# Graph attention over blocks of eight tiles: every third unit's exponent is formed in a PSUM bank, and rows of targets and sides reach all partitions through DRAM

## Chip, cores and metric

One core of one Trainium2 chip. The metric is the device time of one launch, in microseconds (us). Engines: TensorE (PE; PEld is its weight load), VectorE (DVE), ScalarE (ACT), GpSimd (POOL), SyncE (SP, which only issues DMAs here).

## The reference, cut to what matters

6250 nodes with 128 features, 200,000 edges sorted by target. An edge network with a maximum over each target's edges comes first, then a layer norm, then two attention layers of this form (h = x @ W; every node also has an edge to itself), then a layer norm.

```python
a_src = h @ att_src;  a_dst = h @ att_dst
e = a_src[src] + a_dst[dst]
e = jnp.where(e > 0, e, 0.2 * e)
m = segment_max(e, dst)
ex = jnp.exp(e - m[dst])
out = segment_sum(ex[:, None] * h[src], dst) / segment_sum(ex, dst) + bias
```

## The kernel before, in words

The first 2.5 ms are the edge network; the change leaves its loop alone. While it runs, a second thread fills `counts`: edges and nodes are laid out in 62 tiles of 128 targets (rows), and for every tile, every source chunk of 128 nodes and every pair the table holds how many edges join them. So an attention layer has no gather of features: it multiplies dense 128 x 128 tiles of weights by the projected features `tab`.

The 62 tiles go in blocks (`supers`) of 8, the last of 6. A block has 49 **units**, one for each chunk h of 128 sources. Unit u of a block i needs, for 8 x 128 = 1024 target columns at once, exp(max(s + x, 0.2 s + y)), where s is the source's score (one per partition), and x and y are the target's two sides (its score, and 0.2 of it, each less its maximum), as rows that every partition holds: `x_rows`, `y_rows`. Per unit:

- ScalarE, `exponents(u)`: two passes of 1024 columns, exp(x + s) into `e_ring` (L864) and exp(y + 0.2 s) into `f_ring` (L867).
- VectorE, `weigh(u)`: their maximum (L1395); `mask(u)`: capped and multiplied by the counts, into `a_ring`, three deep (L1406).
- TensorE, `add_unit(u)`: eight fp32 products with `tab[:, h]`, added over the 49 units into six PSUM banks, three for each of two blocks in turn (L1758).

Every engine runs its own list, written by loops over u: VectorE weighs u + 1, then masks u. SyncE loads `counts` in pieces of seven units.

Between the units each engine has side work of two kinds, placed by the unit's number h in its block.

*Flushes* of the block before (`flushed`): tile after tile, every five units, TensorE spreads the tile's targets over the partitions (`spread_target`, through the helper at L1559), VectorE compares them (`same_target`, L1416 and L1419), ScalarE copies the tile's sums (`copy_sums`, L873), TensorE adds them up by runs (`sum_runs`, L1777 and L1780), ScalarE copies these (`copy_runs`, L880) and GpSimd stores them. `spread_target` of the next tile waits for `copy_runs`. TensorE's steps are at h = 2 + 5t and 5 + 5t, VectorE's `DVE_AHEAD` and ScalarE's `ACT_AHEAD` units later in their lists.

*Windows* of the block after (`spread_round`, `window_hots`, `copy_round`): SyncE loads `windows`, the sides of 128 consecutive targets per tile, from a table in DRAM (L532). TensorE spreads the targets (helper at L1559), VectorE makes one-hots of them (L1387), TensorE multiplies the two sides, each spread over all partitions, by the one-hots (L1747) and ScalarE copies the results into `x_rows` and `y_rows` (L855): six rounds of four tiles. The sides come in two parts: chunks 0 to 7 before the units, the others in block 0 (`sides_of(1)` after unit 14, `copy_sides(1)`, L1373, after unit 17), because GpSimd gathers the node's maxima one chunk at a time.

## Time and profile before

| | us |
|---|---|
| Median of 3 runs (lowest, highest) | 4994.77 (4974.24, 5006.46) |
| Profiled execution, its own time | 4974.88 |
| Its span | 4973.6 |
| First and last mask, layer 0 | 2730.8, about 3660 |
| First and last mask, layer 1 | 3985.8, 4915.4 |
| Full block of 49 units | 118 to 121 |

| Engine | busy us | share of the span |
|---|---|---|
| PE | 4123.7 | 83% |
| PEld | 3663.1 | 74% |
| DVE | 3968.5 | 80% |
| ACT | 2804.2 | 56% |
| POOL | 2201.4 | 44% |

A row of a group gives the line in the kernel, the engine and operation, out<-in by the program's names, shapes, the count, busy time and mean duration of one, then the idle time of the engine just before such instructions and what ended it. In the stretches, 3330.7 to 3449.9 is block 5 of layer 0 and 3567.6 to 3660.0 its block 7, of six tiles. Durations of neighbours overlap: an instruction's row ends when its results are written, and the next one starts earlier. So the distance between two starts tells what an engine spends on one. An fp32 product is two records on PE.

### The profile page before, as it was taken

To read this page: it belongs to the slowest core of one execution; us is meant where nothing else is said; L and a number is where in the kernel's file an instruction comes from. 1 tells how busy PE (TensorE), PEld (TensorE's weight loads), DVE (VectorE), ACT (ScalarE), POOL (GpSimd) and SP (SyncE) were. 2 spreads that over 40 slices of the span, in tenths; PEclk is the share of its full clock that TensorE was granted. 3 is DMA by queue.
4 is the path that set the end of the run, shared out by engine and by line. 5 is a ranking of instruction groups with operands and counts; after the bars stand their busy time and mean duration, and the time that the engine had idled before them with its cause. 6 is when DMAs were issued, how large, how long until landed. Compare 5 with 4: busy or idle time off the path is not lost. (4 is left out here: it accounts for less than half of the span.)

```text
span 4973.6 us, 98581 instructions
## 1 busy us (share of the span) xinstructions
PE 4123.7 (83%) x35974; PEld 3663.1 (74%) x35974; DVE 3968.5 (80%) x6028; ACT 2804.2 (56%) x3925; POOL 2201.4 (44%) x2117
## 2 busy tenths in 40 slices
PE   4588888888888888888596888888889788888884
PEld 3477777777777777776474888888877578888884
DVE  4477677777677777765685999999978699999998
ACT  2244444444444444443301899999960089999997
POOL 7777777777777777777302100111120120011121
PEclk7799999999999999998797999999999899999997
DMA  5578677778777777777474211222237512222222
GB/s 174 156 201 228 199 212 216 216 210 222 201 215 216 215 211 218 217 204 200 111 238 145 54 57 57 68 61 62 62 69 241 171 46 59 63 61 61 68 58 58
DMA packets 774547, 721.12 MB, mean 145 GB/s; under 512 B 106779, under 2 KB 642387, under 8 KB 774220
## 3 DMA queue, kind: packets, MB, share of 16 engines
q10 hardware_dynamic: 383570, 310.71, 23.0%
q1 hardware_dynamic: 322714, 271.27, 18.4%
q0 software_dynamic: 67936, 135.03, 9.1%
q8 instruction: 174, 2.85, 0.3%
q14 instruction: 153, 1.25, 0.1%
HBM read 539.16 MB, written 177.56 MB: 144 GB/s over the span
## 5 line engine op out<-in xcount | busy, mean ns | idle before, releaser
L599 POOL DMA_INDIRECT ring_a<-Q_table,late x1563 | 1657.9, 1061 | 477.3 <-issue 466.5
L1758 PE MATMUL ps<-tab_flat,ring_b 128*128 128x129 f32 x12152 | 1502.5, 282 | 75.8 <-DVE ring_b L1406 73.3
L1758 PEld LDWEIGHTS ps<-tab_flat,ring_b 128*128 128x128 f32 x12152 | 1438.9, 197 | 117.6 <-DVE ring_b L1406 115.5
L1395 DVE TENSOR_TENSOR work<-work 128x1024 f32<-128x1024 f32 (+1 forms) x784 | 930.4, 1187 | 43.2 <-ACT work L867 39.9
L864 ACT ACTIVATE work<-work,scores 128x1024 f32<-128x1024 f32 (+1 forms) x784 | 879.6, 1122 | 148.6 <-DVE ring_b L1406 125.8
L1406 DVE SCALAR_TENSOR_TENSOR ring_b<-work,ring_a 128x1024 f32<-128x1024 f32 (+1 forms) x784 | 928.1, 1184 | 3.2 <-PE ps L1758 2.7
L1629 PEld LDWEIGHTS ps<-work,tab_flat 128*128 128x128 bf16 x7936 | 795.7, 142 | 179.7 <-issue 174.8
L1629 PE MATMUL ps<-work,tab_flat 128*128 128x49 bf16 x7936 | 875.0, 273 | 0.0
L867 ACT ACTIVATE work<-work,slope_src 128x1024 f32<-128x1024 f32 (+1 forms) x784 | 868.1, 1107 | 0.0
L1144 DVE TENSOR_TENSOR_SCAN work<-ring_b,work,ps 128x512 f32<-128x512 bf16 x391 | 497.9, 1273 | 446.8 <-PE ps L1602 445.1
L1171 DVE TENSOR_TENSOR tab_flat<-digit_of,ring_b 128x1280 bf16<-128x1280 bf16 x806 | 645.3, 801 | 175.3 <-PE ps L1629 174.0
L766 ACT ACTIVATE ring_a<-ps 128x490 uint8<-128x490 f32 x806 | 480.7, 597 | 537.2 <-PE ps L1629 517.7
L656 POOL DMA_DIRECT2D run_rows<-ring_b x124 | 67.7, 546 | 1577.1 <-ACT ring_b L880 1552.9
L1591 PE MATMUL ps<-ident,ring_a 128*128 128x128 f32 x1563 | 462.9, 296 | 350.6 <-issue 187.2
L714 ACT ACTIVATE work<-ps 128x512 f32<-128x512 f32 x392 | 234.3, 598 | 750.1 <-PE ps L1592 744.2
L1592 PE MATMUL ps<-work 128*128 128x128 f32 x3126 | 592.9, 292 | 0.0
L1591 PEld LDWEIGHTS ps<-ident,ring_a 128*128 128x128 f32 x1563 | 237.3, 152 | 396.9 <-issue 308.8
L1592 PEld LDWEIGHTS ps<-work 128*128 128x128 f32 x3126 | 526.6, 211 | 0.3 <-issue 0.3
L1602 PE MATMUL ps<-work,W 128*128 128x512 f32 (+1 forms) x784 | 437.6, 641 | 0.0
L648 POOL DMA_INDIRECT node_tops<-run_tops,end_i x98 | 116.8, 1192 | 536.5 <-DMA run_tops<-late 507.2
L855 ACT ACTIVATE work<-ps 128x512 f32<-128x512 f32 x64 | 36.1, 564 | 524.9 <-PE ps L1747 524.9
L1173 DVE TENSOR_TENSOR work<-column_of,ring_b 128x490 bf16<-128x490 bf16 x806 | 325.0, 403 | 0.0
(267 smaller groups left out, 4475.3 us busy)
## 6 DMA issues: line engine op xcount, KB each, us to landing
work<-low_rows SPq DMA_DIRECT2D x312, 320.0 KB, 4.1
ring_b<-rank_rows ACTq DMA_DIRECT2D x194, 512.0 KB
run_max<-tab_flat ACTq DMA_DIRECT2D x194, 512.0 KB
ring_a<-counts SPq DMA_DIRECT2D x98, 896.0 KB, 5.1
work<-P_compact SPq DMA_DIRECT2D x787, 64.0 KB
work<-P_compact ACTq DMA_DIRECT2D x776, 64.0 KB
counts<-ring_a ACTq DMA_DIRECT2D x62, 784.0 KB
ring_a<-Q_table,late POOLq DMA_INDIRECT x1563
```

The source lines that it names most:

```text
L599: pool.indirect_dma_start(out=q_ring[:, g % RING, j - j0, :], out_offset=None, in_=Q_table, in_offset=bass.IndirectOffsetOnAxis(ap=srcT_i[ ...
L766: scalar.activation(count_tile[:, tau % 2, :, r0:r1], bank[:, 0:(r1 - r0) * NB].rearrange("p (r h) -> p h r", h=NB), ACT.Copy).then_inc(ba ...
L864: scalar.activation(e_ring[:, u % 3, 0:n], x_rows[:, i % 2, 0:n], ACT.Exp, bias=scores[:, h, 0:1])
L867: scalar.activation(f_ring[:, u % 2, 0:n], y_rows[:, i % 2, 0:n], ACT.Exp, bias=slope_src[:, h:h + 1]).then_inc(exped, 1)
L1144: vector.tensor_tensor_scan(scanned[:, b, 0:n * P], b_ring[:, g % RINGB, 1, a * P:(a + n) * P], ps[2 + b][:, 0:n * P], initial, ALU.add, A ...
L1171: vector.tensor_tensor(hot_rows[:, slot, :, 0:r1 - r0], digit_of[:, :, 0:r1 - r0], low_key[:, tau % 2, r0:r1].unsqueeze(1).to_broadcast([P ...
L1395: vector.tensor_tensor(e_ring[:, u % 3, 0:n], e_ring[:, u % 3, 0:n], f_ring[:, u % 2, 0:n], ALU.max).then_inc(weighed, 1)
L1406: vector.scalar_tensor_tensor(out=a_ring[:, u % RINGA, 0:n].rearrange("p (k e) -> p k e", e=P), in0=e_ring[:, u % 3, 0:n].rearrange("p (k ...
L1591: tensor.matmul(piece, lhsT=q_ring[:, g % RING, a + c, :], rhs=ident[:, :], start=True, stop=False, is_transpose=True)
L1592: m = tensor.matmul(piece, lhsT=w_ring[:, g % RING, a + c, :], rhs=onto[:, i % 3, c * P:(c + 1) * P], start=False, stop=True)
L1629: m = tensor.matmul(bank[:, k * NB:(k + 1) * NB], lhsT=hot_rows[:, hot_slot[b], :, k], rhs=hot_cols[:, hot_slot[b], :, k], start=True, sto ...
L1758: m = tensor.matmul(sums_of(tau), lhsT=a_ring[:, u % RINGA, (tau - a) * P:(tau - a + 1) * P], rhs=tab[:, h, 0:F + 1], start=(h == 0 and (t ...
```

## The change

Of the 49 units of a block, those with h = 1, 4, 7, ... (16) are **banked**, the other 33 **direct**.

A *direct* unit uses exp(max(x + 0.8 s, y) + 0.2 s), the same value: VectorE forms x + 0.8 s and the maximum with y in one instruction (`weigh`, two units ahead now), ScalarE does one exp of 1024 columns in place, VectorE masks.

A *banked* unit uses exp(relu(x - y + 0.8 s) + y + 0.2 s). In halves of 512 columns and in PSUM bank 5 alone, ScalarE writes relu (`begin_bank`, L957 of the new kernel), TensorE adds y on all partitions as a product of ones with three bf16 parts of the row y (`add_to_bank`, L1961), and ScalarE writes the exp to SBUF (`exponents_of_bank`, L965); VectorE only masks. Two halves make five turns of the bank, counted by `bank_turned`. The sums of units now use banks 0 to 4, so `copy_sums` takes the first three tiles of a block at once, right after its last unit, and `sums_sb` is three deep.

The windows of blocks 1 to 7: the targets, transposed once and stored to `target_rows`, are loaded to all partitions (`load_targets`); VectorE compares them in SBUF (`equal_targets`) and splits the window's side into three bf16 parts (`split_window`, nine small instructions); TensorE multiplies parts and both sides by the one-hots with five columns of weights (`spread_parts`, L1938); ScalarE copies three rows of parts and, through `row_stage`, stores the two sides to `row_table` (`copy_parts`), from where they are loaded to all partitions (`load_rows`); VectorE subtracts y from x (`split_rows`). Block 0 keeps its six rounds and gets two more for the parts.

In ScalarE's list, in the middle of a block with a window step. Before (L864 and L867 are a unit's two exps):

```order
L867 ACTIVATE work<-work,slope_src 128x1024
L864 ACTIVATE work<-work,scores 128x1024
L867 ACTIVATE work<-work,slope_src 128x1024
L880 ACTIVATE ring_b<-ps 128x129
L864 ACTIVATE work<-work,scores 128x1024
L867 ACTIVATE work<-work,slope_src 128x1024
L873 ACTIVATE ring_b<-ps 128x129
```

And now (L957 relu into the bank, L920 a direct unit's exp, L965 exp out of the bank, L936 and L937 copies of parts and sides, L982 copied runs):

```order
L957 ACTIVATE ps<-work,steep_src 128x512
L920 ACTIVATE work<-work,slope_src 128x1024
L965 ACTIVATE work<-ps,slope_src 128x512
L957 ACTIVATE ps<-work,steep_src 128x512
L920 ACTIVATE work<-work,slope_src 128x1024
L965 ACTIVATE work<-ps,slope_src 128x512
L936 ACTIVATE pair<-ps 3x512
L937 ACTIVATE digit_of<-ps 5x512
L939 DMA row_table<-digit_of 2x512
L982 ACTIVATE ring_b<-ps 128x129
```

Three units are six passes, of which four are halves, where they were six full ones; the second direct unit's exp stands behind the first half's exp.

In TensorE's list, the same block. Before (L1758 units, L1559 a spread, L1777 and L1780 runs, L1747 windows):

```order
L1777 MATMUL ps<-ring_b 128x129
L1780 MATMUL ps<-ring_b 128x129
L1758 MATMUL ps<-tab_flat,ring_b 128x129 x16
L1747 MATMUL ps<-ring_b,windows 128x128 x4
L1559 MATMUL ps<-ident,v_target 128x128
L1758 MATMUL ps<-tab_flat,ring_b 128x129 x24
```

And now (L1951 units, L1961 adds, L1735 a spread, L1979 and L1982 runs, L1938 parts):

```order
L1735 MATMUL ps<-ident,v_target 128x128
L1951 MATMUL ps<-tab_flat,ring_b 128x129 x16
L1961 MATMUL ps<-pair,ones_b 128x512
L1938 MATMUL ps<-ring_b,part_f 5x128 x4
L1951 MATMUL ps<-tab_flat,ring_b 128x129 x8
L1961 MATMUL ps<-pair,ones_b 128x512
L1979 MATMUL ps<-ring_b 128x129
L1982 MATMUL ps<-ring_b 128x129
```

An add stands behind the unit three (second half) or four (first half) ahead of the unit it is for.

In VectorE's list (L1576 masks, L1564 the pass ahead of them, L1586 and L1589 a flush):

```order
L1576 SCALAR_TENSOR_TENSOR ring_b<-ring_b,ring_a 128x1024
L1586 SCALAR_TENSOR_TENSOR ring_b<-ps,v_target,tri 128x128
L1589 SCALAR_TENSOR_TENSOR ring_b<-ps,v_target,last_col 128x128
L1564 SCALAR_TENSOR_TENSOR work<-work,steep_src 128x1024
L1576 SCALAR_TENSOR_TENSOR ring_b<-work,ring_a 128x1024 x2
L1564 SCALAR_TENSOR_TENSOR work<-work,steep_src 128x1024
L1576 SCALAR_TENSOR_TENSOR ring_b<-work,ring_a 128x1024
L1564 SCALAR_TENSOR_TENSOR work<-work,steep_src 128x1024
```

Three units are five passes; before, L1395 and L1406 took turns, six.

The diff, cut to its core:

```diff
-    REST_AT, REST_XY_AT = 14, 16
-    XY_AT, XY_STEP, FLUSH_AT, FLUSH_STEP, ACT_AHEAD, DVE_AHEAD = 4, 4, 2, 5, 6, 3
+    ROUNDS_X, COPIES_X, BANKS, ZBANK, PARTS = 8, 6, 5, 5, 3
+    REST_AT, REST_XY_AT, SPREAD_AT = 14, 18, 46
+    XY_AT, FLUSH_AT, FLUSH_STEP, ACT_AHEAD, DVE_AHEAD = 4, 2, 5, 3, 2
...
+        y_parts = [pair[0:PARTS, 0, 0:FD], digit_a[0:PARTS, 0:FD]]
+
+        def e_slot(u):
+
+            return e_last if u % 4 == 3 else e_first[:, u % 4, :]
...
-            bank = PER * (at % 2) + j // PER
+            bank = (PER * at + j // PER) % BANKS
...
+        def in_bank(u):
+
+            return u % NB % 3 == 1
...
-                    if q - RINGC - 1 < NS:
-                        load_windows_of(q - RINGC - 1)
+                    if q == RINGC + 2:
+                        load_windows_of(1)
+                    elif q > LOADS and q % LOADS == 2 and q // LOADS + 1 < NS:
+                        load_windows_of(q // LOADS + 1)
...
                 def exponents(u):
                     i, h = divmod(u, NB)
                     n = (supers[i][1] - supers[i][0]) * P
-                    if h == 0:
-                        scalar.wait_ge(window_copied, 4 * (layer * NS + i + 1))
-                    if layer or u >= 3:
-                        scalar.wait_ge(masked, unit0 + max(u - 2, 0))
-                    scalar.activation(e_ring[:, u % 3, 0:n], x_rows[:, i % 2, 0:n], ACT.Exp, bias=scores[:, h, 0:1])
-                    if u >= 2:
-                        scalar.wait_ge(weighed, unit0 + u - 1)
-                    scalar.activation(f_ring[:, u % 2, 0:n], y_rows[:, i % 2, 0:n], ACT.Exp, bias=slope_src[:, h:h + 1]).then_inc(exped, 1)
+                    scalar.wait_ge(weighed, layer * NC + direct_until(u + 1))
+                    scalar.activation(e_slot(u)[:, 0:n], e_slot(u)[:, 0:n], ACT.Exp, bias=slope_src[:, h:h + 1]).then_inc(exped, 1)
+
+                def load_targets(i):
+                    first, n = supers[i][0] * P, (supers[i][1] - supers[i][0]) * P
+                    scalar.wait_ge(window_spread, spreads(layer, i))
+                    scalar.dma_start(window_hot.rearrange("p k e -> p (k e)")[:, 0:n],
+                                     target_rows[:, first:first + n].to_broadcast([P, n])).then_inc(targets_landed, 16)
+
+                def copy_parts(i, half):
+                    c, n, at = halves_of(i)[half]
+                    scalar.wait_ge(window_spread, spreads(layer, i) + half + 1)
+                    if half == 0 and i >= 2:
+                        scalar.wait_ge(bank_turned, layer * TURNS + 1 + 5 * banked_until((i - 1) * NB))
+                    scalar.activation(y_parts[i % 2][:, c:c + n], ps[6][0:PARTS, 0:n], ACT.Copy)
+                    scalar.activation(row_stage[:, 0:n], ps[6][0:PARTS + 2, 0:n], ACT.Copy).then_inc(window_copied, 1)
+                    scalar.wait_ge(window_copied, copies(layer, i) + half + 1)
+                    scalar.dma_start(row_table[:, at:at + n], row_stage[PARTS:PARTS + 2, 0:n]).then_inc(rows_stored, 16)
+
+                def load_rows(i, half):
+                    c, n, at = halves_of(i)[half]
+                    scalar.wait_ge(rows_stored, stored(i, half))
+                    if half == 0 and i >= 2:
+                        scalar.wait_ge(weighed, layer * NC + direct_until((i - 1) * NB))
+                    for a, rows in enumerate((x_rows, y_rows)):
+                        scalar.dma_start(rows[:, i % 2, c:c + n], row_table[a:a + 1, at:at + n].to_broadcast([P, n])).then_inc(rows_landed, 16)
+
+                def begin_bank(u, half):
+                    i, h = divmod(u, NB)
+                    columns, n, turns = z_half(u, half)
+                    if half == 0:
+                        scalar.wait_ge(window_split, 2 * (layer * NS + i) + 2)
+                    scalar.wait_ge(bank_turned, layer * TURNS + turns)
+                    if half == 0 and banked_until(u):
+                        scalar.wait_ge(exped, unit0 + max(x for x in range(u) if in_bank(x)) + 1)
+                    scalar.activation(ps[ZBANK][:, 0:n], r_rows[:, i % 2, columns], ACT.Relu, bias=steep_src[:, h:h + 1]).then_inc(bank_turned, 1)
+
+                def exponents_of_bank(u, half):
+                    i, h = divmod(u, NB)
+                    columns, n, turns = z_half(u, half)
+                    if half == 0 and (layer or u >= 4):
+                        scalar.wait_ge(masked, unit0 + max(u - 3, 0))
+                    scalar.wait_ge(bank_turned, layer * TURNS + turns + 2)
+                    one = scalar.activation(e_slot(u)[:, columns], ps[ZBANK][:, 0:n], ACT.Exp, bias=slope_src[:, h:h + 1])
+                    one.then_inc(exped if half else bank_turned, 1)
...
+                    if u == 0:
+                        begin_bank(1, 0)
+                        exponents_of_bank(1, 0)
+                        begin_bank(1, 1)
+                    if u + 2 < UNITS and in_bank(u + 2):
+                        begin_bank(u + 2, 0)
+                    if not in_bank(u):
+                        exponents(u)
+                    if u + 2 < UNITS and in_bank(u + 2):
+                        exponents_of_bank(u + 2, 0)
+                        begin_bank(u + 2, 1)
+                    if u + 1 < UNITS and in_bank(u + 1):
+                        exponents_of_bank(u + 1, 1)
+                    if i and h == 1:
+                        for tau in range(supers[i - 1][0], supers[i - 1][0] + PER):
+                            copy_sums(tau)
+                    if rows_at(i + 1, h) == 0:
+                        load_targets(i + 1)
+                    if rows_at(i + 1, h) == 8:
+                        copy_parts(i + 1, 0)
+                    if rows_at(i + 1, h) == 12:
+                        load_rows(i + 1, 0)
+                        copy_parts(i + 1, 1)
+                    if rows_at(i + 1, h) == 16:
+                        load_rows(i + 1, 1)
...
+                def equal_targets(i):
+
+                    first, e = supers[i]
+                    vector.wait_ge(targets_landed, 16 * (layer * (NS - 1) + i))
+                    for j in range(e - first):
+                        vector.tensor_scalar(window_hot[:, j, :], window_hot[:, j, :], window_col[:, first + j:first + j + 1], None,
+                                             ALU.is_equal).then_inc(dve.up(), 1)
+
+                def split_window(i):
+
+                    first, n = supers[i][0], supers[i][1] - supers[i][0]
+                    column = windows[:, first:first + n, 1]
+                    vector.wait_ge(windows_landed[i % 2], windows_value(layer, i))
+                    if layer or i:
+                        vector.wait_ge(window_spread, spreads(layer, i))
+                    for a in range(PARTS):
+                        rest = part_rest[:, a - 1, 0:n] if a else column
+                        vector.tensor_copy(part_b[:, a, 0:n], rest).then_inc(dve.up(), 1)
+                        vector.wait_ge(dve.sem, dve.n)
+                        one = vector.tensor_copy(part_f[:, 0:n, a], part_b[:, a, 0:n])
+                        if a == 0:
+                            vector.tensor_copy(part_f[:, 0:n, PARTS:PARTS + 2], windows[:, first:first + n, :])
+                        if a + 1 < PARTS:
+                            vector.tensor_tensor(part_rest[:, a, 0:n], rest, part_b[:, a, 0:n], ALU.subtract).then_inc(dve.up(), 1)
+                            vector.wait_ge(dve.sem, dve.n)
+                    one.then_inc(window_split, 1)
+
+                def split_rows(i):
+
+                    n = (supers[i][1] - supers[i][0]) * P
+                    vector.wait_ge(window_copied, copies(layer, i + 1))
+                    if i:
+                        vector.wait_ge(rows_landed, 16 * 4 * (layer * (NS - 1) + i))
+                    if layer or i >= 2:
+                        vector.wait_ge(bank_turned, layer * TURNS + 5 * banked_until(max(i - 1, 0) * NB))
+                    vector.tensor_tensor(r_rows[:, i % 2, 0:n], x_rows[:, i % 2, 0:n], y_rows[:, i % 2, 0:n], ALU.subtract).then_inc(window_split, 1)
...
+                    if in_bank(u):
+                        return
+                    if u >= 4:
+                        vector.wait_ge(masked, unit0 + u - 3)
+                    vector.scalar_tensor_tensor(out=e_slot(u)[:, 0:n], in0=x_rows[:, i % 2, 0:n], scalar=steep_src[:, h:h + 1],
+                                                in1=y_rows[:, i % 2, 0:n], op0=ALU.add, op1=ALU.max).then_inc(weighed, 1)
...
-                    if u + 1 < UNITS:
-                        weigh(u + 1)
+                    if u + 2 < UNITS:
+                        weigh(u + 2)
...
+                    if rows_at(i + 1, h) == 3:
+                        equal_targets(i + 1)
+                        split_window(i + 1)
+                    if i + 1 < NS and h == SPREAD_AT:
+                        split_rows(i + 1)
...
+                def spread_parts(i, half):
+                    c, n, at = halves_of(i)[half]
+                    tensor.wait_ge(window_split, 2 * (layer * NS + i) + 1)
+                    tensor.wait_ge(window_copied, copies(layer, i) + half)
+                    for j in range(n // P):
+                        m = tensor.matmul(ps[6][0:PARTS + 2, j * P:(j + 1) * P], lhsT=part_f[:, c // P + j, :],
+                                          rhs=window_hot[:, c // P + j, :], start=True, stop=True)
...
+                def add_to_bank(u, half):
+                    i = u // NB
+                    columns, n, turns = z_half(u, half)
+                    tensor.wait_ge(bank_turned, layer * TURNS + turns + 1)
+                    tensor.matmul(ps[ZBANK][:, 0:n], lhsT=ones_b[:, :], rhs=y_parts[i % 2][:, columns], start=False, stop=True,
+                                  skip_group_check=True).then_inc(bank_turned, 1)
...
+                    if u + 4 < UNITS and in_bank(u + 4):
+                        add_to_bank(u + 4, 0)
+                    if u + 3 < UNITS and in_bank(u + 3):
+                        add_to_bank(u + 3, 1)
                     if u == REST_AT + 1:
                         turn_sides(1)
-                    if round_at(i + 1, h, 0) is not None:
-                        spread_round(i + 1, round_at(i + 1, h, 0))
+                    if rows_at(i + 1, h) in (5, 9):
+                        spread_parts(i + 1, rows_at(i + 1, h) // 9)
```

## Rows read from the trace of the kernel before

**Rows 1.** The page: busy tenths in 40 slices; granted clock in tenths.
```profile
DVE  4477677777677777765685999999978699999998
...
PEclk7799999999999999998797999999999899999997
```

**Rows 2.** Stretches: us; PE, PEld, DVE, ACT, POOL busy (count); clock, DMA, GB/s.
```profile
3330.70:3449.90 119.20, 106.32 (x883) 102.94 (x882) 119.00 (x124) 110.72 (x120) 14.21 (x15) 0.97 0.22 63
3567.60:3660.00 92.40, 78.70 (x631) 74.90 (x630) 90.55 (x123) 83.12 (x110) 19.01 (x18) 0.96 0.18 50
```

**Rows 3.** Groups, block 5 (3330.7 to 3449.9): busy, mean ns | idle before.
```profile
L1758 PE MATMUL ps<-tab_flat,ring_b 128*128 128x129 f32 x787 | 96.7, 281 | 2.5 <-DVE ring_b L1406 2.5
...
L1395 DVE TENSOR_TENSOR work<-work 128x1024 f32<-128x1024 f32 x50 | 61.1, 1221 | 0.2 <-ACT work L867 0.2
L1406 DVE SCALAR_TENSOR_TENSOR ring_b<-work,ring_a 128x1024 f32<-128x1024 f32 x50 | 60.9, 1217 | 0.0
L864 ACT ACTIVATE work<-work,scores 128x1024 f32<-128x1024 f32 x50 | 57.4, 1149 | 8.6 <-DVE ring_b L1406 6.7
...
L1559 PE MATMUL ps<-ident,v_target 128*128 128x128 f32 x32 | 6.7, 330 | 10.3 <-ACT ring_b L880 10.3
L1747 PE MATMUL ps<-ring_b,windows 128*128 128x128 f32 x32 | 4.2, 275 | 0.0
```

**Rows 4.** Order in time, VectorE: start us, us, instruction.
```profile
3286.53 0.34 DVE L1416 SCALAR_TENSOR_TENSOR ring_b<-ps,v_target,tri 128x128 f32<-128x128 f32 x1
3286.79 0.34 DVE L1419 SCALAR_TENSOR_TENSOR ring_b<-ps,v_target,last_col 128x128 f32<-128x128 f32 x1
3287.05 1.21 DVE L1395 TENSOR_TENSOR work<-work 128x1024 f32<-128x1024 f32 x1
3288.18 1.22 DVE L1406 SCALAR_TENSOR_TENSOR ring_b<-work,ring_a 128x1024 f32<-128x1024 f32 x1
```

**Rows 5.** Order in time, TensorE's records at full clock.
```profile
3308.79 5.52 PE L1758 MATMUL ps<-tab_flat,ring_b 128*128 128x129 f32 x48
3314.15 0.39 PE L1777 MATMUL ps<-ring_b 128*128 128x129 f32 x2
```

**Rows 6.** Order in time, TensorE, a wait for the copied runs.
```profile
3068.81 0.79 PE L1559 MATMUL ps<-ident,v_target 128*128 128x128 f32 x2 [2.16 <-ACT ring_b L880]
```

**Rows 7.** Stretches ahead of and behind that wait's end.
```profile
3060.00:3068.80 8.80, 6.65 (x60) 6.46 (x58) 8.80 (x9) 7.96 (x10) 0.00 (x0) 1.00 0.16 52
3068.90:3072.20 3.30, 3.30 (x16) 3.30 (x17) 3.30 (x5) 3.30 (x5) 0.54 (x1) 0.50 0.06 20
```

**Rows 8.** Order in time, VectorE, layer 0, block 0.
```profile
2768.08 0.20 DVE L1355 TENSOR_TENSOR own_top<-node_tops,negE 128x41 f32<-128x41 f32 x1 [3.54 <-DMA node_tops<-run_tops,end_i]
...
2776.25 0.41 DVE L1373 COPY side_rows<-ps 41x256 f32<-41x256 f32 x1
```

**Rows 9.** Order in time, TensorE's bf16 products in the edge scores.
```profile
2561.71 0.22 PE L1708 MATMUL ps<-src_low_b,work 128*128 128x49 bf16 x1
2561.87 0.38 PE L1702 MATMUL ps<-digit_coef,work 32*128 32x490 bf16 x1
2562.18 0.22 PE L1707 MATMUL ps<-src_high_b,work 128*128 128x49 bf16 x1
```

**Rows 10.** Order in time, ScalarE, a copy of 512 columns out of PSUM.
```profile
3262.08 0.57 ACT L855 ACTIVATE work<-ps 128x512 f32<-128x512 f32 x1
3262.56 0.27 ACT L873 ACTIVATE ring_b<-ps 128x129 f32<-128x129 f32 x1
```

**Rows 11.** DMA issues from 2500 us: count, KB each, us to landing.
```profile
work<-low_rows SPq DMA_DIRECT2D x278, 320.0 KB, 4.1
```

**Rows 12.** Order in time, ScalarE's copies at the start of layer 0.
```profile
2715.16 0.60 ACT L855 ACTIVATE work<-ps 128x512 f32<-128x512 f32 x1 [256.86 <-PE ps L1747]
2717.92 0.60 ACT L855 ACTIVATE work<-ps 128x512 f32<-128x512 f32 x1 [2.16 <-PE ps L1747]
```

**Rows 13.** Order in time, SyncE: windows of block 1.
```profile
2780.99 5.48 SPq L532 DMA_DIRECT2D windows<-side_table  x8
```

135 lines of the change are left out of this document (95 added, 40 removed).

## The prediction

> **What bounds the kernel now.** I read the page first, for where the time lies. In forty slices VectorE stands at 9 tenths in slices 23 to 29 and 33 to 39, the units' parts of the two attention layers, and mostly at 7 or less elsewhere [rows 1]. Then a table of stretches, one per block of eight tiles: 119.2 us, of which VectorE is busy 119.0, TensorE 106.3, ScalarE 110.7 [rows 2]. The last block has six tiles and takes 92.4. Eight blocks in each of two layers; blocks 1 to 6 of a layer are full and have flushes, block 0 has none. Everything outside these blocks I leave as it is: the change adds one transpose, one copy and one small store there, none in a loop.
>
> Then the groups of one block [rows 3]: 50 maxima of 1.22 us and 50 masks of 1.22 us on VectorE are 122 of busy time, more than the stretch, because a row's duration overlaps the next one. The order in time gives the true price: passes start 1.13 us apart, the two small ones of a flushed tile 0.26 each [rows 4]. So 98 x 1.13 + 8 x 0.52 + 8 x 0.26 (the window's hots, of the same shape) = 117.0 of 119.2. **VectorE bounds the blocks**, with 2.2 us of loss.
>
> TensorE is the second: 48 matmul records in 5.36 us [rows 5], 0.112 each (an fp32 product is two records, a unit of 8 tiles 16, so 1.79 us). A block has 784 for units, 48 for flushes, 48 for windows: 880 x 0.112 = 98.6. It waited 10.3 us for ScalarE's copy of the runs and 2.5 us for masks [rows 3]. After one of these waits, of 2.16 us [rows 6], the granted clock was 0.50 for 3.3 us, having been 1.00 [rows 7]. Such spells are the 0.03 missing in the block [rows 2]: 6% of 119 us at half speed, 3.6 us lost.
>
> **The change, part by part, for a full block.**
>
> *VectorE.* 16 of 49 units lose their pass ahead of the mask; the other 33 keep one (an add and a maximum in one instruction, two SBUF operands as the mask's; I price it as the mask, 1.13; the maximum alone lasts the same to 4 ns). 82 x 1.13 = 92.7. Flushes stay 4.2. The hots stay 8, now read from SBUF: 2.1. New are nine small instructions on 8 columns, at most 0.20 each by the nearest row [rows 8]: 1.8, and one full subtraction, 1.13. Sum 101.9, with today's 2.2 of loss 104.1.
>
> *TensorE.* It loses 48 records for windows and gains 16: 848 x 0.112 = 95.0. It gains 32 bf16 products of 512 columns on three rows. The nearest is the one of 490 columns on 32 rows: 0.31 us from its start to the next start, and 0.12 more of a gap before it than its neighbours have [rows 9]. I take 0.30, the bounds are nothing and 0.43: 9.6, between 0 and 13.8. Sum **104.6** at 2.4 GHz, between 95.0 and 108.8. By the Trainium skill, "TensorE: Matmul & The Clock Gate", Part 1, a warm matmul of N = 512 starts 215.7 ns before the next. The adds would then be 6.9 and the sum 101.9; no row here shows it.
>
> *TensorE's waits and clock.* Most of today's 10.3 us wait goes: ScalarE copies a tile's runs at unit 8 + 5t of its list instead of 11 + 5t, and the spread of the next target, at 7 + 5t on TensorE, mostly finds it done. With fewer waits I leave one half-speed spell per block, as the one of 3.3 us (1.7 lost), instead of two. The same page says that the throttled clock is the default and activity releases it; by it nearly all spells would go, as TensorE now hardly pauses, and the block would be 1.7 shorter. The rows agree in direction: 1.00 in the busy stretch, 0.50 right after the wait [rows 6, 7].
>
> *ScalarE.* 33 passes of 1.15 (starting 1.05 apart) and 64 half passes; a half pass out of PSUM lasts 0.57 and lets the next start after 0.48 [rows 10]. Into PSUM no row shows; bounds 0.48 and a full pass. 35 + 31 + 8 flush copies twice (4) + four part copies (2) = 72 of about 109: no bound by itself. Its DMA issues (eight a block: one load, two stores, four loads) I put at nothing, hidden in this slack.
>
> *The chain through the bank.* A banked unit goes ScalarE, TensorE, ScalarE, VectorE, and ScalarE's exponent of the third direct unit is queued behind its first half. So from the mask of unit 3 to that of unit 6: mask 1.22, unit 1.79, add 0.38, half exponent 0.48, half seed 0.48, exponent 1.15, and five hand-overs of about 0.04: **5.7 us for three units**. VectorE needs 5 x 1.13 = 5.65 for the same three, 5.96 with the flushes' share; TensorE 3 x 1.79 + 2 x 0.30 = 5.97, and 6.37 with theirs. All three lie within a tenth. TensorE is the longest, so it becomes the bound, and the chain's 0.3 to 0.6 us of slack decides how well it is fed. VectorE's burst at the window (3.9 us) is more than the two units that TensorE can hold in the mask ring, so some shows. I take 2.7 us of stalls.
>
> Full block: 104.6 + 1.7 + 2.7 = **109.0**, a gain of 10.2.
>
> *DMA.* The target row goes to 128 partitions, 512 KB, asked three units (6 us) before VectorE uses it. The nearest row, 320 KB broadcast in the same way, lands in 4.1 [rows 11]. By size I get 5 to 6.6, so it is covered or up to 1 us late; a counts load on the same queues could make it 4. The rows' two other trips have four units, 8 us, each. At 0 to 3 us a block this stays in the range.
>
> *Block 0.* Nothing before unit 15 is gained: VectorE waits until 2768.08 for gathers that GpSimd issues at its own pace [rows 8]. The new start is about 8 us longer (two more rounds at 2.76 each by [rows 12], a subtraction, the first turns of the bank) and eats the 3.54 us of wait and what 14 units gain. After that 34 units. VectorE: 57 x 1.13 + 5 (window) + 1.5 (sides) = 71. Then a **new wait**: the windows of block 1 are issued from 2780.99 to 2786.47 [rows 13], so landed near 2789, 12.6 us after the copy at 2776.25 [rows 8]. VectorE now wants them four units after that copy, 8.3 us: 4.3 us of wait. With 2.7 of stalls 78, instead of 84 from there to block 1: gain 6.
>
> *Last block.* Passes of 768 columns: today 92.4 [rows 2]. TensorE 588 + 48 + 24 records = 74, adds 7, clock 1: 82. Gain 10.
>
> Per layer 6 x 10.2 + 6 + 10 = 77, twice is 154. The profiled execution lasted 4974.9, so 4821. The median of the runs stands 20 us above it and their spread is 32; I add half of that offset: **4830**.
>
> **Rivals.**
>
> *A, my forecast: TensorE bounds*, 106 to 112 a full block, 4780 to 4865. For it: the sums above. Against: it rests on 0.30 for an add that no row shows. Chance 0.58.
>
> *B, the chain sets the pace.* If every flush step falls on it, three units take 5.7 + 0.31 + 0.40 + 0.26 (VectorE's, TensorE's, ScalarE's shares) = 6.67; 16.3 such triples are 109, and VectorE's bursts of 5 us come on top: 114. Gain 2 x (6 x 5.2 + 2 + 6) = 78: 4897. For it: no engine has slack and every queue is strictly in order. Against: TensorE can hold two units in reserve. Chance 0.19.
>
> *C, VectorE stays the bound*: 104.1 a block, if adds cost 0.22 or less and no slow spell is left. The skill's two statements above would bring TensorE to 101.9, below VectorE, and so make this one. Gain 2 x (6 x 15.1 + 9 + 13) = 225: 4750. Chance 0.12.
>
> *D, slower: the turns of the bank are dear.* One bank serves every banked unit, five turns each, none of which overlaps another. A block equals today's 119.2 when three units take 7.3 us. B's chain with its bursts stands at 7.0. So 0.1 us more at each of the four hand-overs between ScalarE and TensorE, or a seed into PSUM that lasts 0.5 longer, is enough. With 0.6 more on the chain it is 7.6 a triple, 124 a block, and 4975 + 2 x (6 x 4.8 + 6) = 5045. For it: no row shows a ScalarE write into PSUM. Against: reads out of it are cheaper per start than SBUF's passes. Chance 0.06. The Trainium skill ("ScalarE: Activation LUTs", Step-by-step) says the opposite, that PSUM is its faster destination; that alone leaves A, B and C as they are.
>
> *E, the gain is lost elsewhere*: late landings in each block on top of B, 4930 to 5020. Chance 0.05.
>
> **Numbers.** One per cent, about what a measurement of this kernel can tell from no change, is 50 us. A and C and most of B lie below 4945: faster 0.86. Same 0.08 (the end of B, and E), slower 0.06. The range leaves out D, E and the tips of C and B: 4750 to 4920.
>
> **What would show it.** Right: full blocks of 107 to 111 us with TensorE's records over 95 of it back to back, its wait for the copied runs nearly gone, VectorE idle some 4 to 6 us a block for exponents or for summed units, a start-to-start distance of the adds near 0.30, granted clock of 0.98 or above, one VectorE wait for windows of about 4 us in block 0. Wrong: TensorE idle ahead of units by more than 8 us a block while VectorE waits for ScalarE (B), VectorE without waits and blocks of 104 (C), half passes into PSUM above 0.8 us or ScalarE waiting for TensorE at each add by more than a unit's time (D), VectorE waiting for the target rows' DMA in every block (E).

## Result, and the profile after

| | before | after |
|---|---|---|
| Median, us (lowest, highest), 4 runs each | 4996.89 (4974.24, 5006.46) | 4937.01 (4931.03, 4954.32) |
| Ratio, with its 95% interval | | 0.989 [0.985, 0.993] |
| Profiled execution, us | 4974.88 | 4931.03 |
| Full block (blocks 1 to 5 of both layers) | 118.9 to 119.9 | 115.3 to 115.7 |

The change made the kernel 60 us faster, 1.1%. The forecast was 4830, with a range from 4750 to 4920, a gain of some 165.

The page's slices, with VectorE and the granted clock:

```profile
DVE  4477677777777677776577699899978779999998
...
PEclk7799999999999999999699799999999989999998
```

VectorE still reads 9 tenths in most of the units' slices, as before [rows 1]. A slice of 123 us and a digit of a tenth don't show the change; a table of stretches does. The stretches of block 0, block 5 and block 7 of layer 0, with the columns of [rows 2]:

```profile
2749.00:2866.70 117.70, 109.06 (x818) 96.06 (x818) 102.08 (x108) 79.81 (x101) 16.37 (x13) 0.95 0.23 62
3328.80:3444.10 115.30, 112.22 (x881) 99.65 (x880) 104.56 (x117) 82.65 (x117) 14.54 (x15) 1.00 0.27 79
3557.90:3646.70 88.80, 86.60 (x667) 76.49 (x667) 79.45 (x109) 64.26 (x109) 14.80 (x15) 1.00 0.18 51
```

Block 5 takes 115.3 where it took 119.2. TensorE is busy for 112.2 and VectorE for 104.6, so they have changed places. The clock is 1.00, where it was 0.97. From the first to the last mask the last block takes 88.7 instead of 93.4 (its stretch of 92.4 in [rows 2] ends 1 us before the last mask), block 0, whose clock is 0.95, 117.7 instead of 121.3 from its first mask to that of block 1.

Groups of block 5, as [rows 3]:

```profile
L1951 PE MATMUL ps<-tab_flat,ring_b 128*128 128x129 f32 x784 | 96.6, 278 | 3.1 <-DVE ring_b L1576 3.1
...
L1576 DVE SCALAR_TENSOR_TENSOR ring_b<-work,ring_a 128x1024 f32<-128x1024 f32 x37 | 44.8, 1222 | 7.3 <-issue 6.6 <-ACT work L920 0.6
L1564 DVE SCALAR_TENSOR_TENSOR work<-work,steep_src 128x1024 f32<-128x1024 f32 x26 | 33.2, 1278 | 0.0
...
L957 ACT ACTIVATE ps<-work,steep_src 128x512 f32<-128x512 f32 x32 | 22.2, 693 | 4.8 <-DVE work L1555 3.2 <-ACT digit_of L937 0.4
L965 ACT ACTIVATE work<-ps,slope_src 128x512 f32<-128x512 f32 x23 | 15.7, 683 | 18.9 <-PE ps L1961 18.9
...
L1961 PE MATMUL ps<-digit_a,ones_b 3*128 3x512 bf16 x31 | 11.9, 385 | 0.0
```

And its waits (engine, tile and line, what was waited for; us, times, the longest):

```profile
ACT work L965 <- PE ps L1961: 18.9, 16, 2.5
DVE ring_b L1576 <- issue: 8.4, 11, 1.4
ACT ring_b L965 <- PE ps L1961: 7.3, 5, 2.0
...
PE ps L1951 <- DVE ring_b L1576: 3.1, 6, 1.1
```

TensorE's wait of 10.3 us for the copied runs has gone. VectorE's masks wait 8.4 us by the row of the waits (rows that say "issue"), and ScalarE stands 26 us ahead of the exps out of the bank. How this hangs together is seen in order of time, all engines:

```profile
3300.60 1.87 PEld L1951 LDWEIGHTS ps<-tab_flat,ring_b 128*128 128x128 f32 x16
3300.71 1.95 PE L1951 MATMUL ps<-tab_flat,ring_b 128*128 128x129 f32 x16
...
3302.59 0.09 PEld L1961 LDWEIGHTS ps<-pair,ones_b 3*128 3x128 bf16 x1
3302.59 0.38 PE L1961 MATMUL ps<-pair,ones_b 3*128 3x512 bf16 x1
3302.91 1.86 PEld L1951 LDWEIGHTS ps<-tab_flat,ring_b 128*128 128x128 f32 x16 [0.23 <-issue]
3302.91 2.05 PE L1951 MATMUL ps<-tab_flat,ring_b 128*128 128x129 f32 x16
3303.08 0.69 ACT L965 ACTIVATE work<-ps,slope_src 128x512 f32<-128x512 f32 x1 [1.90 <-PE ps L1961]
...
3303.80 0.69 ACT L957 ACTIVATE ps<-work,steep_src 128x512 f32<-128x512 f32 x1
...
3304.58 1.14 ACT L920 ACTIVATE ring_b<-ring_b,slope_src 128x1024 f32<-128x1024 f32 x1
...
3305.81 1.23 DVE L1576 SCALAR_TENSOR_TENSOR ring_b<-ring_b,ring_a 128x1024 f32<-128x1024 f32 x1 [1.10 <-issue]
```

The add starts at 3302.59. ScalarE has stood for 1.90 us for it; then it does this half's exp, the next relu, a copy (not shown) and only at 3304.58 the exp of a direct unit, which reads nothing of the bank. VectorE has stood for 1.10 us when it starts the mask of that direct unit (3305.81). The rows on PE tell what an add costs. Within a unit records start 0.112 apart; to the add it is 0.208, from the add to the next record 0.315. The second record behind the add is late as well: 16 records last 2.05 us in the row behind the add, 1.95 in the row of the unit before, and their weight load, which began 0.11 ahead of the products in the unit before (3300.60), starts with them at 3302.91. These three, 0.096 and 0.315 and 0.10, are the same at nearly all of the 32 adds of block 5 that no wait touches: an add costs **0.51 us**, 16.3 in a block. With 848 x 0.112 = 95.0 the sum is 111.3, and 4.1 us of 115.4 are left for waits.

### The profile page after: what moved, and what is told of

Same layout as the page of the kernel before. It is cut to its first block and busy times, and to the rows that moved or that the text cites. A ratio compares the mean times of both kernels' runs of the same rounds, so it can differ in the third digit from the quotient of the medians.

```text
span 4929.7 us, 99359 instructions
## 1 busy us (share of the span) xinstructions
PE 4243.3 (86%) x36089; PEld 3633.6 (74%) x36089; DVE 3747.7 (76%) x5936; ACT 2372.8 (48%) x3913; POOL 2191.1 (44%) x2117
## 5 line engine op out<-in xcount | busy, mean ns | idle before, releaser
L1951 PE MATMUL ps<-tab_flat,ring_b 128*128 128x129 f32 x12152 | 1512.2, 279 | 57.9 <-DVE ring_b L1576 57.9
L1951 PEld LDWEIGHTS ps<-tab_flat,ring_b 128*128 128x128 f32 x12152 | 1412.7, 192 | 153.5 <-DVE ring_b L1576 89.6
L1576 DVE SCALAR_TENSOR_TENSOR ring_b<-work,ring_a 128x1024 f32<-128x1024 f32 (+1 forms) x588 | 691.8, 1189 | 122.7 <-issue 97.0
L771 ACT ACTIVATE work<-ps 128x512 f32<-128x512 f32 x392 | 234.4, 598 | 761.7 <-PE ps L1769 760.9
L1564 DVE SCALAR_TENSOR_TENSOR work<-work,steep_src 128x1024 f32<-128x1024 f32 (+1 forms) x396 | 493.3, 1246 | 0.0
L920 ACT ACTIVATE work<-work,slope_src 128x1024 f32<-128x1024 f32 (+1 forms) x396 | 439.8, 1111 | 12.2 <-DVE work L1564 9.0
L965 ACT ACTIVATE work<-ps,slope_src 128x512 f32<-128x512 f32 (+1 forms) x384 | 256.5, 668 | 309.4 <-PE ps L1961 296.8
L957 ACT ACTIVATE ps<-work,steep_src 128x512 f32<-128x512 f32 (+1 forms) x512 | 347.7, 679 | 75.5 <-DVE work L1555 44.4
L705 POOL DMA_INDIRECT node_tops<-run_tops,end_i x98 | 102.6, 1046 | 530.5 <-DMA run_tops<-late 501.2
```

The source lines that it names most:

```text
L920: scalar.activation(e_slot(u)[:, 0:n], e_slot(u)[:, 0:n], ACT.Exp, bias=slope_src[:, h:h + 1]).then_inc(exped, 1)
L1564: vector.scalar_tensor_tensor(out=e_slot(u)[:, 0:n], in0=x_rows[:, i % 2, 0:n], scalar=steep_src[:, h:h + 1], in1=y_rows[:, i % 2, 0:n], o ...
L1576: vector.scalar_tensor_tensor(out=a_ring[:, u % RINGA, 0:n].rearrange("p (k e) -> p k e", e=P), in0=e_slot(u)[:, 0:n].rearrange("p (k e) - ...
L1951: m = tensor.matmul(sums_of(tau), lhsT=a_ring[:, u % RINGA, (tau - a) * P:(tau - a + 1) * P], rhs=tab[:, h, 0:F + 1], start=(h == 0 and (t ...
```

## Experiments

The quantity compared is the full block, from the start of its first mask to that of the next block's. Given is the median of blocks 1 to 5 of both layers. Most of these ten agree within 0.4 us (single blocks of e3 and e8 are 1.1 longer), where whole times move by some 30 us with the edge network ahead of the layers. Every experiment is one run, e9 five, so whole times are given for the record and the argument goes by blocks. Four runs (e8, e11, e12 twice) were on two other chips, where the first mask came some 410 to 430 us later; the kernel before took 5445 and 5449 there. Their full blocks can be compared all the same: a mask lasts the same 1.22 us, and the run with 32 rows repeats the changed kernel's busy times in block 5 to 0.1.

**Rows of the adds (e3).** The adds use three rows of weights. Here all 128 are used, with weights of zero beyond the third; the other rows of the moving operand keep what these tiles held before, finite numbers, so the product is the same.

```diff
-        ones_b = sb("ones_b", [PARTS, P], BF16)
+        ones_b = sb("ones_b", [P, P], BF16)
+        y_wide = [pair[:, 0, 0:FD], digit_a[:, 0:FD]]
...
-                    vector.memset(ones_b[:, :], 1.0).then_inc(dve.up(), 1)
+                    vector.memset(ones_b[:, :], 0.0).then_inc(dve.up(), 1)
+                    vector.wait_ge(dve.sem, dve.n)
+                    vector.memset(ones_b[0:PARTS, :], 1.0).then_inc(dve.up(), 1)
...
-                    tensor.matmul(ps[ZBANK][:, 0:n], lhsT=ones_b[:, :], rhs=y_parts[i % 2][:, columns], ...
+                    tensor.matmul(ps[ZBANK][:, 0:n], lhsT=ones_b[:, :], rhs=y_wide[i % 2][:, columns], ...
```

> The changed kernel whose adds have 128 rows of weights (ones in the first three rows, zeros in the others) and 128 rows of moving data, the same result. In the changed kernel an add starts 0.208 us after the last unit record ahead of it (0.096 more than the usual 0.112) and the next record starts 0.315 after the add. If the few rows keep the weight loads on either side from being hidden (theory R), the add falls to about 0.22 + 0.11: 32 x 0.2 = 6 us less on TensorE, and under theory T a block takes 109 to 111. If the change of number format, bf16 between fp32, is the cause (theory F), the distances stay and a block stays at 115.4.

Measured: 4871.4 (before 4989.1), full block 110.7. The stretch, then the weight loads around an add:

```profile
3310.40:3421.10 110.70, 105.75 (x882) 99.44 (x881) 104.18 (x118) 82.33 (x117) 14.10 (x15) 1.00 0.31 82
...
3305.92 0.64 PEld L1954 LDWEIGHTS ps<-tab_flat,ring_b 128*128 128x128 f32 x5
3306.56 0.10 PEld L1964 LDWEIGHTS ps<-digit_a,ones_b 128*128 128x128 bf16 x1
```

And TensorE's records around an add of this kernel:

```profile
3300.04 0.38 PE L1964 MATMUL ps<-pair,ones_b 128*128 128x512 bf16 x1
3300.25 1.95 PE L1954 MATMUL ps<-tab_flat,ring_b 128*128 128x129 f32 x16
3302.36 2.05 PE L1954 MATMUL ps<-tab_flat,ring_b 128*128 128x129 f32 x16 [0.16 <-DVE ring_b L1579]
```

The add's weight load (3306.56, line 1964) now starts ahead of its product at 3306.59; with three rows both started at 3302.59, after the product before. From the add to the next record it is 0.216, to the add 0.112, and 16 records behind it last 1.95 again. So an add costs 0.216, and 32 cost 6.9 instead of 16.3. The forecast for few rows as the cause came (109 to 111); with the number format as the cause nothing would have changed. The block became 4.6 shorter, and not 9.4, because what is left beside the records grew from 4.1 to 8.8: the chain through the bank is next, as e9 shows.

The last row shows one thing more: 16 records last 2.05 us behind a wait too, with no add ahead of them. The kernel before has the same: in blocks 1 to 6 of layer 0, at full clock, the second record behind each of TensorE's 90 waits of over 0.3 us starts 0.21 after the first. So the third mark of an add is not its own; it stands wherever the stream of records starts anew.

Is it the number of rows, or that they are not all? The same with 64 and with 32 rows, in place of 128:

```diff
-        ones_b = sb("ones_b", [P, P], BF16)
+        ones_b = sb("ones_b", [64, P], BF16)
...
-        y_wide = [pair[:, 0, 0:FD], digit_a[:, 0:FD]]
+        y_wide = [pair[0:64, 0, 0:FD], digit_a[0:64, 0:FD]]
```

> The adds with 64 rows of weights and of the moving operand (three of them filled as before, 61 of weights zero), in place of 3 in the changed kernel (add 0.41 us, full block 115.4) and 128 in the run e3_rows128 (0.22 and 110.7). Theory W (any product that does not use all 128 rows has its weights loaded only after the product before it, and holds up the load behind it in the same way): distances 0.208 before and 0.315 behind an add, block 115.4. Theory N (the cost goes with the number of rows left out): half of the difference, 0.16 before and 0.265 behind, block near 113.

> The same with 32 rows, the number of the edge scores' product in the kernel before. Theory W: 0.208 and 0.315, block 115.4, as with 3 rows. Theory N: 0.18 and 0.29, block near 114.3.

Measured: 5396.0 and 5378.0 (before 5448.6), full blocks 115.4 and 115.4; an add with 64 rows in order of time, and the two stretches:

```profile
3761.67 0.39 PE L1964 MATMUL ps<-digit_a,ones_b 64*128 64x512 bf16 x1
3761.99 1.86 PEld L1954 LDWEIGHTS ps<-tab_flat,ring_b 128*128 128x128 f32 x16 [0.23 <-issue]
3761.99 2.05 PE L1954 MATMUL ps<-tab_flat,ring_b 128*128 128x129 f32 x16
```

```profile
3755.50:3870.90 115.40, 112.33 (x881) 99.70 (x880) 104.61 (x118) 82.70 (x117) 14.77 (x15) 1.00 0.27 79
```

```profile
3738.20:3853.50 115.30, 112.22 (x881) 99.65 (x880) 104.56 (x117) 82.64 (x117) 14.54 (x15) 1.00 0.27 79
```

From the add to the next record 0.32 again, and the row behind it is 2.05 long. Theory W holds for the numbers tried: 3, 32 and 64 rows cost the same, 128 rows less than half; nothing between 64 and 128 was run. (The 0.41 in these expectations is the sum of the two distances next to the add, 0.096 and 0.315; the second late record, 0.10, makes it 0.51.)

**ScalarE's order (e2).** The second direct unit's exp goes ahead of the first half's exp out of the bank:

```diff
-                    if u + 2 < UNITS and in_bank(u + 2):
-                        exponents_of_bank(u + 2, 0)
-                        begin_bank(u + 2, 1)
                     if u + 1 < UNITS and in_bank(u + 1):
+                        if u:
+                            exponents_of_bank(u + 1, 0)
+                            begin_bank(u + 1, 1)
                         exponents_of_bank(u + 1, 1)
```

> The changed kernel with ScalarE's list reordered: the exponent of a direct unit stands before the first half's exponent of the banked unit, not behind it. The chain mask 3, unit 3, add, half exponent, half seed, exponent 6, mask 6 is cut: exponent 6 no longer waits for TensorE. Work on each engine is the same. Theory T (TensorE's list bounds, 108.1 of 115.4 a block): at most part of the 7 us of waits goes, 112 to 115. Theory C (the chain sets the pace): 105 to 110, VectorE's own sum of about 104 being next.

Measured: 4872.4 (before 4989.1), full block 111.4. The stretch, and TensorE's units in it:

```profile
3308.50:3419.90 111.40, 111.40 (x882) 99.51 (x880) 104.32 (x117) 82.87 (x117) 14.75 (x15) 1.00 0.30 82
...
L1951 PE MATMUL ps<-tab_flat,ring_b 128*128 128x129 f32 x786 | 96.5, 278 | 0.0
```

TensorE is busy for all 111.4 and its units have no idle ahead of them; the sum of its records was 111.3. So these 4 us were waits that came of the place of one exp in ScalarE's list, and nothing but TensorE's own work is left. The result lies between what the two theories gave (112 to 115 and 105 to 110) and in neither: both had the adds at 0.41, so TensorE's sum at 108.1 and 7 us of waits.

**Is it TensorE's length or the chain?** Two more records of 124 columns, 16 times in a block (16 x 2 x 0.112 = 3.6 us), into columns of a bank that nobody reads, ahead of units whose end no add follows (e1) or ahead of units with h = 3, 6, ..., which an add follows (e11):

```diff
+                    if h % 3 == 2:                  # e11: if h and h % 3 == 0
+                        spare_bank = ps[PER * i % BANKS]
+                        tensor.matmul(spare_bank[:, 388:512], lhsT=a_ring[:, u % RINGA, 0:P],
+                                      rhs=tab[:, h, 0:124], start=False, stop=True, skip_group_check=True)
```

> The changed kernel with one extra fp32 product (two records of 124 columns, into columns of the block's first sums bank that nothing uses) ahead of each unit with h = 2, 5, 8, ... (16 a block). These units are not on the way from a mask to the next exponent through the bank: between the first half's add (behind unit 3) and the mask of unit 6 TensorE's unit 5 is waited for by nobody. A full block takes 115.4 us now. Theory T, TensorE's own list is the bound (848 records at 0.112 = 95.0, 32 adds at 0.41 = 13.1, 7 of waits): the extra 32 records at 0.112 = 3.6 us show nearly in full, 118 to 119 a block. Theory C, the chain through the bank sets the pace and TensorE has room: 115.4 to 116.2.

> The changed kernel with the extra product of e1_pad moved onto the chain: ahead of each unit with h = 3, 6, 9, ... (16 a block), that is between a mask and the add that ScalarE waits for before it can form the exponent of the next such unit. The same 3.6 us of TensorE's time. Off the chain (e1_pad) a block grew by 2.5 from 115.4. If TensorE's list alone sets the pace the place does not matter: 117.8 again. If the chain carries part of the time: 118.5 to 119.5.

Measured: e1 4966.0 (before 4989.1), full block 117.8, 2.5 longer, 69% of what was put in. e11 5429.7 (before 5444.8), full block 118.0, 2.7 longer, 75%.

```profile
3336.20:3454.00 117.80, 115.82 (x913) 103.24 (x912) 104.65 (x117) 82.55 (x117) 13.84 (x15) 1.00 0.27 78
```

```profile
3754.40:3872.40 118.00, 115.80 (x913) 103.21 (x912) 104.73 (x117) 82.54 (x117) 13.57 (x15) 1.00 0.27 77
```

Where the work is put makes little difference, so its length counts: TensorE bounds the block. The rest went into its waits, 4.1 before. With room on TensorE e1 was to take 115.4 to 116.2, which did not come; its 118 to 119 was missed by 0.2, and e11's 118.0 lies between its two forecasts.

**Fewer banked units**, every fourth, 12 a block, alone (e4) and with ScalarE's new order (e8):

```diff
-            return u % NB % 3 == 1
+            return u % NB % 4 == 1
```

> The changed kernel with 12 banked units a block (every fourth, the first of them h = 1; 13 where the count of 49 gives it) instead of 16. TensorE: 94.7 + 26 x 0.41 + 3.3 = 108.6; VectorE: 49 x 1.13 + 36 x 1.20 + 8.7 + 2 = 109.3; the chain is stretched over four units. Theory T alone (TensorE's list plus waits in proportion to banked units): 111 to 113. Theory C (the chain binds three units together, 7.06 us a turn): with four units a turn it is off the path and VectorE bounds, 109 to 111. Both below 115.4: fewer banked units are faster than the 16 of the change as it stands.

> e4_every4 (12 banked units, adds as in the change, 113.8 a block) with the order of e2_order. TensorE's list is 94.7 + 24 x 0.41 + 3.3 = 107.9, VectorE's 49 x 1.13 + 37 x 1.20 + 8.7 + 2 = 110.5. If the waits that remained in e4_every4 (about 6 us on TensorE) came from ScalarE's order, they go and a block is 110 to 111. If they came from somewhere else: 113 to 114.

Measured: e4 4894.2 (before 4980.6), full block 113.8; e8 5322.8 (before 5444.8), 110.5.

```profile
3303.20:3417.00 113.80, 109.07 (x873) 98.66 (x872) 108.88 (x122) 76.13 (x105) 13.95 (x15) 1.00 0.29 80
```

```profile
3734.50:3846.00 111.50, 107.97 (x873) 98.33 (x872) 108.28 (x121) 77.04 (x105) 14.04 (x15) 1.00 0.30 82
```

(e8's full blocks are 110.2 to 110.5 but for the one in this row, block 5.) With 24 adds the same price gives 95.0 + 12.2 = 107.2. e4 then has 6.6 us of waits, and misses what was expected of it: fewer adds had been expected to bring fewer waits too, and they brought more. The new order halves them, to 3.3, as was expected of e8; VectorE's own sum is then 49 x 1.13 + 37 x 1.19 + 8.8 = 108.2, more than TensorE's 107.2.

**No banked unit (e5)**: all 49 direct.

```diff
-            return u % NB % 3 == 1
+            return False
```

> The changed kernel with no banked unit: all 49 of a block are direct, the rows still come through DRAM. TensorE has 848 records and no adds: 95.0 us. VectorE has 98 passes: 49 masks at 1.13, 49 of the new first pass, which starts 1.20 before the next, and 4.2 + 1.6 + 1.8 + 1.1 of side work = 123. Both theories expect 123 to 126 a block and ScalarE below 60 percent: slower than the 119.3 of the kernel before, so that all that the change gains comes from the banked units and the moved windows give back nothing.

Measured: 5039.5 (before 4989.1), full block 122.4. The stretch, and the pass ahead of the masks:

```profile
3362.50:3484.90 122.40, 107.46 (x850) 100.05 (x850) 122.23 (x134) 61.45 (x70) 19.17 (x15) 0.97 0.26 74
...
L1560 DVE SCALAR_TENSOR_TENSOR work<-work,steep_src 128x1024 f32<-128x1024 f32 x37 | 47.8, 1293 | 0.0
```

VectorE is busy throughout, and the block is just under the 123 expected. The new windows, rows through DRAM and the direct form cost 3 us a block by themselves; what the kernel gained is all from the banked units. It also prices the new pass. 122.4 less 49 masks at 1.13, flushes 4.2, hots 1.65, the small ones 1.8 and a subtraction of 1.14 leaves 58.2 for 49, 1.19 each.

**Both edits**, 128 rows and ScalarE's order, and the same with the pad of e1:

> ScalarE's order of e2_order and the adds of e3_rows128 together. Either alone took a full block from 115.4 to 111.4 and to 110.7 us. TensorE's list is then 848 records at 0.112 (94.7), 32 adds at about 0.22 (7.0) and some 3 us at the switches: 105; VectorE's 49 x 1.13 + 33 x 1.20 + 8.7 = 103.6, with 2 of loss 105.6. Theory T+C (TensorE's list, and on top of it waits through the chain, both now shorter): 105 to 107 a block, 4790 to 4820 us in all. If the two edits had removed the same waits (theory S, one cause under two names), a block would stay at 109 to 111 and the whole at 4860.

> e9_both with the extra product of e1_pad ahead of 16 units a block (3.6 us of TensorE's time off the chain). In e1_pad a block grew by 2.5. If TensorE's list is what bounds e9_both, a block grows by 3 to 3.6 over e9_both's; if VectorE's passes or the chain bound it, by under 1.5.

Measured: e9 **4772.3** (4761.7 to 4779.5), before 4980.6, ratio 0.9575 [0.9547, 0.9604]; full block 105.5. e10 4819.6, full block 107.2.

```profile
3274.40:3379.80 105.40, 103.00 (x882) 99.72 (x881) 103.41 (x117) 82.80 (x117) 14.52 (x15) 1.00 0.32 87
...
ACT work L966 <- PE ps L1964: 10.5, 18, 1.3
...
PE ps L1954 <- DVE ring_b L1579: 2.3, 3, 1.4
```

```profile
3296.20:3403.50 107.30, 106.47 (x914) 103.51 (x913) 103.89 (x118) 82.91 (x117) 14.74 (x15) 1.00 0.32 85
```

e9 beats both kernels, by 4.2% against the one before. TensorE's sum is 95.0 + 6.9 = 101.9, VectorE's, with the 1.19 of the run above, 33 x 1.19 + 49 x 1.13 and the rest 103.4, both within 4 us of the block. The block is in the range of theory T+C (105 to 107) and outside that of one cause under two names (109 to 111); the whole, 4772, is less than the 4790 to 4820 expected. The pad cost 1.8, 49%, between the two forecasts (under 1.5, 3 or more): VectorE is now about as much the bound as TensorE.

## Why the prediction was wrong

Forecast was a full block of 109.0: 104.6 of TensorE's records, 1.7 for half-speed clock, 2.7 of waits. Measured was 115.4: 111.3, 0 and 4.1.

- **The bound: right.** TensorE's records and VectorE changed places (112.2 and 104.6 busy), and work added to TensorE lengthens the block by 69 to 75% of its length. Rival A's mechanism came, beyond its own time and outside 106 to 112. Rival B's 114 a block is nearer to 115.4, but its sign, TensorE idle ahead of units by more than 8 us a block, did not come (3.1); its chain is real, as 4 us of waits on top of TensorE's sum.
- **The step that failed: the price of an add.** Taken was 0.30, with 0.43 as the upper bound; it is 0.51, 16.3 us a block instead of 9.6. Of the 6.4 us by which the block was missed this makes 6.7; waits add 1.4 and the clock takes 1.7 off. The row used [rows 9] had both marks of a product that does not use all rows, a larger distance ahead of it (0.12 more) and 0.31 behind it. I put the value below their sum, and the second record behind the add, also late by 0.10, was in no bound. That row could not show it (the two products behind its 490 columns start 0.04 apart, as all of their kind), but the late second record behind TensorE's waits in the kernel before could have. The sign that was named, a distance near 0.30 from the add to the next start, came (0.315), and still the price was wrong. The runs with 3, 32, 64 and 128 rows show the cause.
- **"TensorE: Matmul & The Clock Gate", Part 1** in the Trainium skill gives 215.7 ns between products of 512 columns. The run with 128 rows shows 0.216. With fewer rows this case's traces show 0.51 for the add as a whole, so the page's figure is right for the product and not for its neighbours' weight loads. With it the prediction's rival C had TensorE at 101.9, as e9 has with the measured 0.216, and VectorE as the bound at about 104 and 4750 us. The change as it stands was far from that; e9, with all rows and another order too, gave 105.5 and 4772.
- **Waits: 4.1 for 2.7.** Seen was the chain of three units, and that the second direct exp stands behind the first half's. Not seen was that it need not; moving it took all 4. (The three lengths that the prediction put within a tenth, 5.7, 5.96 and 6.37, are 12% apart.)
- **Clock: 0 for 1.7.** In full blocks the granted clock is 1.00; one spell a block was left in the forecast. By the rule of the Trainium skill ("TensorE: Matmul & The Clock Gate", Part 1), that activity releases the throttled clock, nearly all of them would go; by that rule, the trace agrees.
- **VectorE: 103.4 for 101.9** without its waits. The pass with an add and a maximum has starts 1.19 apart, not 1.13; the hots from SBUF are cheaper (0.196 apart, forecast 0.26).
- **Half passes.** The relu into the bank lasts 0.69 (no row showed one; 0.48 or more was taken from start to start, it is 0.63; the exp out of the bank takes 0.72 where the next relu waits for its end). Rival D, with its bank turns half a microsecond dearer, did not come: ScalarE's half passes are 0.15 to 0.24 dearer and the block is below 119.2.
- **DMA: right.** VectorE never waits for the target rows in a full block. Rival E did not come. (ScalarE issues seven DMAs a block, not eight: one, two and four.)
- **Start and block 0: 1.6 lost instead of 6 gained.** The start got 5.2 longer, not 8: from the first of VectorE's small steps behind the gathers (2714.44, before 2701.38) to the first mask it was 29.4 and is 34.6. Its end:

```profile
2742.42 1.23 DVE L1555 TENSOR_TENSOR work<-work 128x1024 f32<-128x1024 f32 x1 [14.70 <-ACT pair L912]
...
2749.00 1.23 DVE L1576 SCALAR_TENSOR_TENSOR ring_b<-work,ring_a 128x1024 f32<-128x1024 f32 x1 [2.96 <-ACT work L920]
```

Block 0 itself gained only 3.6. The wait for windows is there, with 1.5 us instead of 4.3, behind a burst of hots:

```profile
2797.32 1.65 DVE L1525 TENSOR_SCALAR ring_b<-ring_b,window_col 128x128 f32<-128x128 f32 x8
2800.51 0.17 DVE L1537 CAST part_b<-windows 128x8 bf16<-128x8 f32 x1 [1.53 <-DMA windows<-side_table]
```

TensorE ran dry of masks behind this burst, and then had its only half-speed spell among the units of this layer (granted clock 0.50 from 2804.3 to 2808.0):

```profile
2799.51 0.39 PE L1961 MATMUL ps<-pair,ones_b 3*128 3x512 bf16 x1
2804.30 3.81 PE L1951 MATMUL ps<-tab_flat,ring_b 128*128 128x129 f32 x16 [4.40 <-DVE ring_b L1576]
2808.04 0.60 PE L1961 MATMUL ps<-pair,ones_b 3*128 3x512 bf16 x1
```

16 records take 3.7 us behind that wait, 1.9 more than at full clock. So 6 us are lost at this place; the forecast gave VectorE's sum, 71, for the 34 units behind the gathers, 4.3 for the windows and 2.7 for other waits. From the end of the gathers (2780.85) to block 1 it was 85.9, forecast 78. The adds' price alone does not explain it: the run with 128 rows takes 85.3 there, the one with ScalarE's order 83.3, both together 81.1. What makes up the rest was not taken apart.
- **Last block: gain 4.7 instead of 10** (93.4 and 88.7, from the first to the last mask), again the adds, in the main: 660 records are 74, and the adds were put at 7; with 128 rows the block takes 84.7.

In layer 0 blocks 1 to 6 gained 24.4, the start and block 0 lost 1.6, the last block gained 4.7; layer 1 is alike (23.8, 1.5 gained, 4.3), and together it is 57 instead of 154. Of the 97 missed, 74 are in the full blocks, 12 at the starts and blocks 0, 11 in the last blocks. The profiled executions differ by 44, for the edge network's part ended 13.1 us later in the second, and the change leaves its loop alone: in the runs of these experiments, the four with the later first mask left aside, the first side of layer 0 comes between 2695 and 2724.

## What to carry to other kernels

A small matrix product that is put into a stream of full ones should use all 128 rows, with weights of zero where there is nothing to add: here 125 rows of zero weights took the price of an add from 0.51 us to 0.22 and cost one memset more. Where an engine's list is in order, put what depends on nothing new ahead of what waits for another engine: one such exchange was worth 4 us in 115, and together with the rows it was 10. When a mechanism is only known from one row, take the whole disturbance in that row, ahead and behind, as the value and not as the upper bound, and look elsewhere in the trace for what happens to the second instruction behind a break.

## What the runs showed of the hardware

- A product with weights of 3, 32 or 64 rows between full ones of 128: its weight load starts with the product itself, and so does the full load behind it. It is 0.208 us to such a product instead of 0.112, 0.315 from it instead of 0.216, and another 0.10 at the second record after, which stands behind a wait of TensorE as well. The flush products behind such an add show the same (two records 0.214 apart instead of 0.112).
- Few columns of weights do much the same as few rows: the windows' products, with 128 rows and only five columns, start 0.31 behind an add with 128 rows (a full product 0.216) and 0.11 from each other, and the full product behind the last of them comes after 0.200, its second record after 0.214 more (e3 and e9, wherever no wait falls between). No run shows what filling up their columns would give.
- On ScalarE, 512 columns with a bias last 0.68 us out of PSUM (Exp) and 0.69 into it (Relu), where a copy of 512 columns out of it lasted 0.57 [rows 10].
- On VectorE, a maximum with an addition in one instruction lasts 1.278 us for 1024 columns, a maximum alone 1.22 [rows 3]; comparisons of 128 columns start 0.196 apart out of SBUF (blocks 1 to 7 of the new kernel) and 0.259 out of PSUM (the kernel before, the same instruction).
